# A state-space layer and a quantised residual block on one core: chunk products on all 128 partitions by VectorE alone, and chunk states as sums over chunks in place of a recursion

## The reference

```python
dt = jax.nn.softplus(dt + dt_bias)          # one per token and head
xconv = silu(4-tap causal convolution of xBC)   # gives xs, Bm, Cm
def step(hstate, inp):
    xt, dtt, Bt, Ct = inp
    dA = jnp.exp(dtt * A)
    hstate = hstate * dA[:, :, None, None] + dtt[:, :, None, None] * xt[..., None] * Bt[:, None, None, :]
    y = jnp.einsum('bhpn,bn->bhp', hstate, Ct)
    return (hstate, y)
y = (y + D * xh).reshape(...) * silu(z)
y = y * jax.lax.rsqrt(jnp.mean(y * y, axis=-1, keepdims=True) + EPS) * norm_w
out = concatenate([silu(z0) * x0, y]) @ out_proj_w.T
return out * sigmoid(relu(out.mean(...) @ se_w1.T + se_b1) @ se_w2.T + se_b2)
```

## Time and profile before

| | |
|---|---|
| median of 3 runs | 95.99 us (95.42 to 97.13) |
| span of the profiled execution | 95.6 us |
| around that span, against the median | 0.4 us |
| instructions | 1495 |
| DVE busy | 78.9 us (83%) |
| PE busy | 71.7 us (75%) |
| POOL busy | 48.4 us (51%) |
| ACT busy | 38.2 us (40%) |

### The profile page before, as it was taken

The page is one execution under the profiler, slowest core; times in us unless marked ns, Lnnn a source line. Parts: engine busy times, 40 slices in busy tenths (PEclk is TensorE's granted clock), DMA queues, the critical chain, the costliest instruction groups (busy, mean ns, idle before and its releaser), DMA issues.

```text
span 95.6 us, 1495 instructions
## 1 busy us (share of the span) xinstructions
PE 71.7 (75%) x541; PEld 45.1 (47%) x541; DVE 78.9 (83%) x179; ACT 38.2 (40%) x66; POOL 48.4 (51%) x62
## 2 busy tenths in 40 slices
PE   4964599996055938999068161999999999979980
PEld 1331593233031813553053041988899864455460
DVE  4797959369999999998999999668988697999350
ACT  0994002499982940445102006301339250184300
POOL 7928993036594005708999998987770000500000
PEclk9999855799995555579975965599999999999999
DMA  2998000000000000000000000000000000000023
GB/s 46 359 319 327 8 0 0 0 0 3 0 0 7 0 0 0 0 0 0 0 0 0 7 0 3 0 7 0 0 0 3 0 7 0 0 0 3 0 107 112
DMA packets 1736, 3.15 MB, mean 33 GB/s; under 512 B 192, under 2 KB 576, under 8 KB 1728
## 3 DMA queue, kind: packets, MB, share of 16 engines
...
q10 hardware_dynamic: 576, 1.20, 3.4%
...
HBM read 2.53 MB, written 0.52 MB: 32 GB/s over the span
## 4 chain that ended last, share of the span: by engine, by line
PE 43%; DVE 41%; issue 4%; DMA 3%; ACT 3%; POOLq 1%; POOL 1%; DVEq 0%
PE ps L558 9%; DVE mm L939 7%; DVE ell L880 6%; PE ps L305 4%; DMA x_sb<-x_in 3%; PE ps L469 3%; PE ps L295 3%; DVE x L924 3%; PE ps L348 3%; PE ps L277 2%; DVE rem L842 2%; DVE cc L825 2%; DVE htmp L955 2%; PE ps L530 2%; PE ps L496 2%
## 5 line engine op out<-in xcount | busy, mean ns | idle before, releaser
L277 PE MATMUL ps<-zbf 128*128 128x512 bf16 x48 | 12.6, 416 | 1.4 <-DVE zbf L757 1.4
L1177 POOL TENSOR_TENSOR mm<-ell,gsb 64x1024 f32<-64x1024 f32 x4 | 10.2, 2546 | 3.7 <-issue 3.3
L880 DVE TENSOR_TENSOR_SCAN ell<-ps,delta 128x512 f32<-128x512 f32 x8 | 9.3, 1210 | 0.1
L939 DVE TENSOR_TENSOR mm<-ell,gsb 64x1024 f32<-64x1024 f32 x4 | 9.1, 2292 | 0.0
L558 PE MATMUL ps<-h,wk 128*128 128x256 bf16 (+1 forms) x54 | 8.3, 313 | 0.7 <-DVE h L1069 0.7
L277 PEld LDWEIGHTS ps<-zbf 128*128 128x128 bf16 x48 | 5.0, 110 | 7.0 <-issue 1.9
L342 PE MATMUL ps<-rows,sel 96*128 96x128 bf16 x32 | 4.7, 297 | 4.1 <-DVE ell L880 2.1
L558 PEld LDWEIGHTS ps<-h,wk 128*128 128x128 bf16 x54 | 5.1, 97 | 4.1 <-issue 1.4
L1143 POOL TENSOR_TENSOR bc<-bc,btap 128x506 f32<-128x506 f32 (+2 forms) x3 | 3.4, 1139 | 6.5 <-ACT btap L604 5.6
L444 PE MATMUL ps<-mm,xdz 128*32 128x128 f32 x128 | 4.9, 298 | 2.3 <-DVE mm L939 2.0
L342 PEld LDWEIGHTS ps<-rows,sel 96*128 96x128 bf16 x32 | 2.6, 126 | 7.8 <-DVE ell L880 4.3
...
## 6 DMA issues: line engine op xcount, KB each, us to landing
...
```

The lines of the kernel that those rows point to most:

```text
L277: mul(ps[:, bank, :], zbf[:, 0:P], zbf[:, :], start=True, stop=True)
L880: vec_.tensor_tensor_scan(dst, ps[:, SPREAD[g % 2], :], delta[:, :], 0.0, ALU.mult, ALU.add).then_inc(scanned, 1)
L939: tt(mm[0:64, i4, :, 0, :], ell[0:64, j, :, b, :, :], g, ALU.mult).then_inc(m_dve, 1)
L1177: gp.tensor_tensor(mm[64:P, i4, :, 1, :], ell[64:P, j, :, b, :, :], g, ALU.mult).then_inc(m_pool, 1)
```

## The change

**What it does.** Four parts.

1. *Block products.* `mm` loses its zero half: it is 16 tiles of 4 heads by 64 columns. DVE does all of it, 4 instructions on 128 partitions (L920 of the changed kernel); POOL's four are gone, and so are the four `memset` of `mm`. `inside(j, b)` now has 32 matmuls, of 64 rows and 64 columns, in place of 16 of 128 rows and 128 columns; the two chunks of a pair go to two banks.
2. *Log-decay sums.* After dt, PE multiplies it (`dtp`, dt times A) by three triangular masks (`upto`, `after`, `after2`, made by POOL with `affine_select`) into sums of logs; ACT takes one exp of all of them into `lx` (128 x 192). DVE makes two small products with dt (`dl1`, `dl23`). The scan `prow`, `emr`, and the tables `pt` and `eb` are gone.
3. *States.* `x2a` and `x2b` are x (still in PSUM) times those products, three instructions for each j in place of two. The states before chunks 1, 2 and 3 are then 32 matmuls that accumulate over chunks in one bank; ACT copies them to `hc`. The copy, the decays and adds, `hblk` and its `memset` are gone.
4. *Products with C.* `csilu` is used as it stands, 32 rows at a time: 32 matmuls of 64 columns for B and C (L365), 24 for C and the states (L476). `cblk`, its clearing and its four activations are gone; one activation makes `csilu`. `decayed` has two instructions for each j, `from_states` 6 matmuls, `gated_y` three instructions.

The table of constants that is loaded is 416 columns wide, not 576. The core of the diff:

```diff
@@ PE, before the z projection
+            pe.wait_ge(dt_arg, 1)
+            pe.wait_ge(masks_ready, 1)
+            pe.wait_ge(dt_ready, 1)
+            mul(sums[:, L_PRE:L_PRE + IH], upto[:, :], dtp[:, :], start=True, stop=True)
+            mul(sums[:, L_1:L_1 + IH], after[:, :], dtp[:, :], start=True, stop=True)
+            mul(pairs[:, 0], after2[:, :], by_k[:, :, 0, :], start=True, stop=True)
+            mul(pairs[:, 1], after2[:, :], by_k[:, :, 0, :], start=True, stop=False)
+            mul(pairs[:, 1], half_ones[:, 0:1].broadcast_to([P, P]), by_k[:, :, 1, :], start=False, stop=True).then_inc(sums_ready, 1)
...
+            pe.wait_ge(lx_ready, 1)
             pe.wait_ge(parts_ready, 2)
@@ PE, products of B and C
-            def inner_products(b, c):
-                k, c2 = divmod(c, 2)
-                return mul(ps[64 * c2:64 * c2 + 64, GB[b], 256 * k:256 * k + 256], bc[:, b, CHUNK * c:CHUNK * c + CHUNK],
-                           cblk[:, b, c, :, :], start=True, stop=True)
+            def inner_products(q):
+                h, j = divmod(q, 2)
+                s = slice(32 * q, 32 * q + 32)
+                for b in range(2):
+                    for c in range(4):
+                        k, c2 = divmod(c, 2)
+                        t = slice(CHUNK * c, CHUNK * c + CHUNK)
+                        col = CHUNK * (4 * b + 2 * k + h)
+                        last = mul(ps[64 * c2:64 * c2 + 64, GB[j], col:col + CHUNK], bc[s, b, t], csilu[s, b, t],
+                                   start=True, stop=True, tile_position=(32 * q, 64 * c2))
+                last.then_inc(g_half if h == 0 else g_ready, 1)
...
-            inner_pair(0)
+            for q in range(2):
+                inner_products(q)
+            for j in range(2):
+                pe.wait_ge(g_half, j + 1)
+                inner_products(2 + j)
             spread_rows(6)
-            inner_pair(1)
             spread_rows(7)
             x_to_tokens(1)
-            inner_pair(2)
-            inner_pair(3)
@@ PE, states
+            gate_x(1)
+            pe.wait_ge(x2_ready, 6)
...
+                    for c in (1, 2):
+                        mul(o[:, c], bt[:, 2 * b, q, :], x2b[:, c - 1, 2 * j + b, h, :], start=(b == 0 and c == 1), stop=False)
...
+                    for c in (0, 2):
+                        k = c // 2
+                        last = mul(o[:, c], bt[0:CH, 2 * b + k, q, :], x2a[:, tile(j, b, k, h), :, :], start=False,
+                                   stop=(b == 1 and c == 2), tile_position=(0, 32 * q))
@@ PE, inside (c2 is a fifth loop, the outermost)
-                                mul(ps[q0:q0 + 32, YA[j], col:col + P], xdz[:, i, head, :, :], mm[:, i, head, :, :],
-                                    start=(b, k, e) == (0, 0, 0), stop=False)
+                                    mul(ps[q0:q0 + 32, YA[j][c2], col:col + CHUNK], xdz[s, i, head, :, :], mm[s, i, head, :],
+                                        start=(b, k, e) == (0, 0, 0), stop=False, tile_position=(64 * c2, q0))
@@ ACT
+            act.wait_ge(sums_ready, 1)
+            go(lx[:, :], ps[:, DTB, CHUNK:CHUNK + L_N], ACT.Exp, scale=-1.0).then_inc(lx_ready, 1)
             for k in range(1, TAPS - 1):
                 go(btap[:, k, :, :], b_src, ACT.Copy, scale=vc[:, V_CWB + k:V_CWB + k + 1]).then_inc(b_tap, 1)
...
+            act.wait_ge(s_ready, 1)
+            go(hc[:, :, :, :].rearrange("p c b e -> p (c b e)"), ps[:, HB, 0:6 * CH], ACT.Copy).then_inc(h_ready, 1)
@@ DVE, before the copy of the rows
+            dve.wait_ge(lx_ready, 1)
+            tt(dl1[0:CH, :], dt[0:CH, :], lx[0:CH, L_1:L_1 + IH], ALU.mult)
+            tt(dl23[:, :, :, :], dt_k0.unsqueeze(1).broadcast_to([P, 2, 4, 8]),
+               lx[:, L_2:L_N].rearrange("p (z m e) -> p z m e", z=2, e=8), ALU.mult).then_inc(dl_ready, 1)
+            dve.wait_ge(dl_ready, 1)
+            seal(tt(sc[:, 6:8], sc[:, 6:8], sc[:, 6:8], ALU.mult))
             dve.wait_ge(row_ready, 1)
@@ DVE, block products
-                g = gsb[0:64, i4, :].unsqueeze(2).broadcast_to([64, 4, HEADS, CHUNK])
-                tt(mm[0:64, i4, :, 0, :], ell[0:64, j, :, b, :, :], g, ALU.mult).then_inc(m_dve, 1)
+                g = gsb[:, i4, :].unsqueeze(2).broadcast_to([P, 4, HEADS, CHUNK])
+                tt(mm[:, i4, :, :], ell[:, j, :, b, :, :], g, ALU.mult).then_inc(m_ready, 1)
@@ POOL, start
-            seal(gp.memset(mm[0:64, TILES // 2:TILES, :, 1, :], 0.0))
-            seal(gp.memset(mm[64:P, 0:TILES // 2, :, 0, :], 0.0))
+            seal(gp.memset(onesq[:, :], 1.0))
...
-            gp.memset(mm[64:P, TILES // 2:TILES, :, 0, :], 0.0).then_inc(zero_mm, 1)
-            pool.wait_ge(zero_mm, 1)
...
             pool.wait_ge(delta_ready, 1)
+            gp.affine_select(upto[:, :], half_ones, [[1, P]], ALU.is_ge, 0.0, base=0, channel_multiplier=-1)
+            gp.affine_select(after[:, :], half_ones, [[-1, P]], ALU.is_gt, 0.0, base=0, channel_multiplier=1)
+            gp.affine_select(after2[:, :], onesq[:, :], [[-1, P]], ALU.is_gt, 0.0, base=0, channel_multiplier=1).then_inc(masks_ready, 1)
```

315 lines of the change are left out of this document (120 added, 195 removed).

## The result

The changed kernel took 92.39 us as a median of 5 runs (92.18 to 95.38), the kernel before 95.99 us (95.42 to 97.71): a ratio of 0.964 with a 95% interval of 0.959 to 0.970. That is 3.6 us gained where 9.7 were forecast, and the time lies outside the range, above it. The profiled execution is the slowest of the five: 95.38 us, with a span of 93.6 us; its accounts are made against the profiled span before, 95.6 us, so they must explain 2.0 us. Medians here are over all executions; the ratios with an interval compare only executions close to the fastest of each kernel, so they can differ from the ratio of two medians.

A forecast was written before the change was run, and what follows sets the result against it. No engine is full; the chain runs through PE, then DVE, with DVE and POOL taking turns. 1.8 + 0.5 - 2.1 + 9.6 - 0.1 = 9.7 us gained; 95.6 - 9.7 + 0.4 = 86.3 us, range 82.8 to 90.8.

The forecast's parts named there:

- Start: Up to 21 us: without POOL's memset of mm, DVE's first u and PE's dt matmuls come earlier; 1.8 us gained.
- Taps and rows: 21 to 31 us: scan and emr gone, small products added, POOL's additions pushed back by 0.8 us; 0.5 us gained.
- B by C: 31 to 41 us: all 32 small matmuls stand ahead of spread 6, so DVE's seventh scan waits; 2.1 us lost.
- 1.5 to 2.5 named as the sign: B by C: DVE idle this many us in front of its seventh scan, put down to PE's spread.
- S to the gated output: From DVE's first product of x by dt (S) to the gated output: 13.8 us for 23.45, 9.6 us gained.
- the idle 1.5 us named as a sign: States: DVE idle for some 1.5 us in front of its first decay, waiting for C by states.
- The rest: From the gated output on nothing is touched; gated_y has one instruction more, 0.1 us lost.
- The last 0.4 us: Added at the end of the sum as the distance from the profiled span, 95.6 us, to the median of the runs.
- the first one: Rival: early gains don't come, DVE/POOL collisions do, B by C at its upper bound; 91.2 at worst, about 89.5; chance 0.17.
- PE's clock stays up: Rival: less idle at the start and dense PE from S + 4.4 keep the clock high; about 83.7 us; chance 0.15.
- PE becomes the bound: Rival: small fp32 tiles in states and inside don't overlap, time rises; 98.5 us at 60 ns a record; chance 0.04.
- Each change of tile shape empties PE: Rival: from S on, about ten tile-shape changes each cost 0.28 us; 89.1 us; chance 0.08.

The follow-up runs named there:

- t3: Changed kernel plus full-size zero matmuls at s1's places, ahead of rows and spreads 0 and 2 to 5, and between the dt matmul halves: 86.95 us.
- u1: t3 with DVE's removed recursion put back as a stand-in on scratch, PE waiting for it ahead of C by states: 98.12 us.
- u2: t3 with POOL's four removed block products put back as a stand-in into scratch: 91.73 us.
- u0_after_again: The changed kernel again, no edit: median 95.09 us, ratio 0.959 to the kernel before; its profile is of a 92.47 us execution.
- s1: Changed kernel plus 15 full-size bf16 zero matmuls on PE, three behind each of the four inside products and C by states: 90.87 us, ratio 0.926 to before.
- t2: Changed kernel with s1's 15 zero matmuls in the same places, but on a 64 x 32 tile: 102.25 us.
- w1: t3 with a memset and two additions on scratch on DVE ahead of its first product of x by dt, PE's wait left empty: 98.78 us.

## Why the prediction was wrong, by its own steps

- **Start, 1.8 us gained:** partly. The first u was undisturbed, as forecast; the two u end at 11.7 us, the second behind `sel` (1.98 us), as named. But both u started 0.76 us later than before (9.42 for 8.66 us), and PE's dt matmuls at 10.39 us, not near 9.2: they stood behind the eight zero products of PE's warm-up, which took 3.33 us for 1.89 before. The first scan comes at 29.61, 1.1 us ahead of the earlier trace rows where start and taps together promised 2.3. PE's L307 (3.21 us for four projections, at 0.5) shows where the rest went: the clock fell in the start all the same. The three `affine_select` took 0.29 to 0.30 us each, far below the 1.2 of the nearest row.
- **Taps and rows, 0.5 us:** the L842 pair went from 2.37 to 0.45 us, and two casts behind it collided instead (1.29 and 1.28 us), the mishap that the step had named at 1 us. Start and taps together are over by 1.2 us.
- **B by C, 2.1 us lost:** the mechanism was right, the size less. From the first scan to S it was 10.83 us and is 12.34, so 1.5 lost; DVE waits 1.02 us in front of its seventh scan, below the 1.5 to 2.5 named as the sign, and 0.68 in front of its second. The 64 records took 2.73 us for an estimate of 3.5.
- **S to the gated output, 23.45 to 13.8 us:** the sum is right, 14.1 us, from 41.95 to 56.06; two of its terms are not, and they cancel. POOL's gate product held the block products up (4.54 us for three), the fourth took 1.21, and PE's states came at S + 4.1 for a forecast of S + 4.4. C by states began at S + 6.1 for S + 8.2 and ended at S + 8.8 for S + 11.3, with the clock still high; DVE's first decay, which needs only its first half, began at S + 8.4 for S + 10.4, without the idle 1.5 us named as a sign. From the end of C by states to the gated output it then took 5.3 us for a forecast of 2.5: the clock had fallen, and `from_states(0)`, put at 0.3 us, took 1.9 (1.10 at the high clock in t3). The sum put it at 0.3 although show 1.10 us for its counterpart before (L478). That 14.1 met 13.8 is luck to this extent. u1 puts 3.8 us of the gain on the recursion. A collision with POOL isn't shown to be a price in the changed kernel: with POOL's products put back beside it in u2, the layer stayed as long as it was.
- **The rest, 0.1 us lost. This is the step that failed:** "From there on nothing is touched." The instructions are untouched, but not their durations. The tail took 37.5 us in the profile after and 34.3 in u0_after_again, in the place of 30.6. The 27th slice and all behind it in the earlier trace rows show 9, and the sum took these rows' durations as given, though the 9.4 us ahead of them (S + 4.4 to S + 13.8) were to be filled with some 320 matmul records on small tiles. s1 and t3 show that it is the clock (34.2 and 31.5 us with the late fills in), and t2 that fills on small tiles don't hold it. What drops the clock in the changed kernel stays open, as said above.
- **The last 0.4 us.** The sum ends with the distance from the profiled span to the median, and front and forecast take 0.4 for it. Every execution whose span is listed took 1.67 to 1.91 us more than its span (95.38 and 93.6 here). So the profiled execution before took an estimated 97.4 us, and its span was set against a median of quicker ones: 1.3 us of the miss.
- **The miss of 6.1 us added up**, with u0_after_again (92.47 us) for the median: 3.6 behind the gated output, 1.3 from the last term, 1.2 in start and taps, 0.7 in the layer, less 0.6 at B by C. That is 6.2.
- **The rivals.** Half of the losses of the first one would give 88.8 us, not the 89.5 that it states. "PE's clock stays up" knew that the clock decides but gave it only an upside, 83.7 us at 0.15; its mirror image, that the clock falls later and longer than before, had no rival, and it is what happened. "PE becomes the bound" saw that PE would be on the chain from S on, and priced it by records, at 58 ns each; `inside` took 5.5 us for 256 records, 22 ns each, mostly at the low clock. "Each change of tile shape empties PE": the page's rule on a drain (the Trainium skill, "TensorEngine Tiling (Array Packing)", Key Properties) isn't seen. The chain shown above has L436 on 128 x 32 tiles (46.11 + 0.62) and L443 on 64 x 32 (46.73), L476 on 32 x 64 (49.36 + 1.41) and L458 on 64 x 32 (50.77), L458 (53.02 + 1.10) and L491 on 64 x 128 (54.13), each behind the other with 0.01 us and less between, so the trace shows no price of a drain at these changes; the ends of matmuls are modelled in it.

The clock's page in the Trainium skill ("TensorE: Matmul & The Clock Gate", Part 1) says that the lower clock is the state that the array is in unless activity lifts it. The traces agree with that where PE is empty (in w1 the clock falls within the wait of 2.77 us), but t2 has PE full in the profile, 18.00 of 18.00 us, at 0.52: what the profile calls busy isn't what lifts it.
